# A decoder kernel on one core: transposes of the feature stage get a PSUM bank of their own, the constant fills of a scratch area are issued in another order, and the causal row maxima take one instruction

## What is computed

```python
x = x + linear_attention(layernorm(x))     # "stage 0": q, k, v projections, then
#   dd  = einsum('bhnd,md->bhnm', data * d**-0.25, proj)      m = 32 features per head
#   qf  = exp(dd_q - 0.5*|q|^2 - max over m of dd_q) + 1e-4
#   kf  = exp(dd_k - 0.5*|k|^2 - max over everything) + 1e-4
#   out = (qf @ (kf^T v)) / (qf @ sum kf)
x = x + cross_attention(layernorm(x), ctx, mask)              # "stage 1", softmax
x = x + tree_feed_forward(layernorm(x))                       # routed leaves, gathered by row
x = x + causal_attention(layernorm(x))                        # "stage 2", softmax
x = x + cross_attention(layernorm(x), ctx)                    # "stage 3", softmax
x = x + expert_layer(layernorm(x))                            # top 16 of 1024 per head
```

## Time and profile before

| | us |
|---|---|
| median of 3 runs (888.3 to 891.41) | 890.37 |
| the profiled execution | 889.77 |
| its span, first to last instruction | 887.7 |
| busy: PE 700.2 (79%), DVE 640.8 (72%), ACT 440.9 (50%), POOL 280.0 (32%) | |

### The profile page before, as it was taken

One profiled execution on the slowest core, in us unless ns is written; L12 is line 12 of the kernel. 1 busy time (PEld: TensorE's weight loads), 2 busy tenths in 40 slices (PEclk: granted clock), 3 DMA queues, 4 the chain that ended last, 5 costly groups with the idle time before them and its releaser, 6 DMA issues. The chain is left out here.

```text
span 887.7 us, 15168 instructions
## 1 busy us (share of the span) xinstructions
PE 700.2 (79%) x5016; PEld 533.6 (60%) x5016; DVE 640.8 (72%) x2791; ACT 440.9 (50%) x1051; POOL 280.0 (32%) x253
## 2 busy tenths in 40 slices
PE   3876877887657988987777588888876958888898
PEld 1435533444257767776675466555456947877788
DVE  5675547653499698976795456776449999999984
ACT  1113003465067787888762345555632556455562
POOL 3012732201333132331240111211012037677793
PEclk9887557998678999999887689988987989999999
DMA  8500051300489887997546233332000000000000
GB/s 256 139 1 2 0 72 29 41 14 1 170 326 354 328 330 266 372 401 262 207 168 166 60 44 47 48 39 39 3 1 1 1 1 2 4 4 4 7 4 7
DMA packets 42678, 93.67 MB, mean 106 GB/s; under 512 B 4050, under 2 KB 30194, under 8 KB 34408
## 3 DMA queue, kind: packets, MB, share of 16 engines
q0 software_dynamic: 9216, 69.47, 20.5%
q1 hardware_dynamic: 33384, 23.23, 13.0%
HBM read 74.42 MB, written 0.52 MB: 84 GB/s over the span
## 5 line engine op out<-in xcount | busy, mean ns | idle before, releaser
L757 ACT ACTIVATE arena<-arena,hact 128x128 f32<-128x128 f32 x512 | 155.0, 388 | 1.0
L567 POOL TENSOR_TENSOR arena<-arena 128x1024 f32<-128x1024 f32 x64 | 121.2, 1914 | 82.6 <-DVE arena L1227 65.2
L657 ACT ACTIVATE arena<-psum 128x512 f32<-128x512 f32 (+1 forms) x192 | 102.8, 561 | 86.5 <-PE psum L1377 85.4
L888 DVE TENSOR_REDUCE rowmax<-psum 128x2 f32<-128x512 f32 x128 | 82.6, 688 | 35.1 <-PE psum L1359 32.8
L1078 DVE CUSTOM_DVE_ANT_0 arena<-arena,fx 128x128 f32<-128x128 f32 x384 | 106.0, 350 | 0.3
L1700 PE MATMUL psum<-arena 128*128 128x128 f32 x688 | 87.3, 285 | 21.3 <-DVE arena L1227 19.2
L1700 PEld LDWEIGHTS psum<-arena 128*128 128x128 f32 x688 | 82.8, 199 | 24.5 <-DVE arena L1227 12.9
L1359 PE MATMUL psum<-arena 128*128 128x256 bf16 (+1 forms) x384 | 79.4, 307 | 22.6 <-DMA arena<-parts 12.3
L1589 PE MATMUL psum<-identf,arena 128*128 128x128 f32 x544 | 75.0, 292 | 25.4 <-ACT arena L757 25.2
L810 ACT ACTIVATE psum<-arena,tneg 128x1024 f32<-128x1024 f32 x64 | 71.0, 1112 | 39.7 <-POOL arena L567 14.0
L1589 PE MATMUL psum<-arena,identf 128*128 128x128 f32 x544 | 78.6, 299 | 15.4 <-ACT arena L757 14.6
(11 more groups left out here) (220 smaller groups left out, 1219.9 us busy)
## 6 DMA issues: line engine op xcount, KB each, us to landing
arena<-parts SPq DMA_DIRECT2D x144, 64.0 KB
arena<-zeros SPq DMA_DIRECT2D x6, 1232.0 KB
w_sb<-attn_w SPq DMA_DIRECT2D x1, 768.0 KB, 7.8
x<-x_in SPq DMA_DIRECT2D x1, 512.0 KB, 4.3
fx<-ctx_in SPq DMA_DIRECT2D x1, 512.0 KB, 4.9
picked<-mask_in SPq DMA_DIRECT2D x1, 512.0 KB, 6.1
wq_sb<-peer_wq SPq DMA_DIRECT2D x1, 512.0 KB, 7.9
down_sb<-table_down SPq DMA_DIRECT2D x1, 512.0 KB, 8.6
```

Source lines behind the costliest of these rows:

```text
L567: nc.gpsimd.tensor_tensor(grid[k % 3].rearrange("p (i j) -> p i j", i=PK), sim[:, t, h, :].unsqueeze(2).to_broadcast([P, PK, PK]), sim[:, ...
L657: nc.scalar.activation(probs[k % (2 * HG)][:, 0:w], bank(2 + k % 2, 0, w), ACT.Exp, scale=float(D) ** -0.5).then_inc(probs_ready, 1)
L757: a = nc.scalar.activation(w, w, ACT.Copy, scale=hact[i % 2][:, l:l + 1])
L888: i = nc.vector.tensor_reduce(rowmax[n % 2][:, :, h], bank(k % 2).rearrange("p (s n) -> p s n", s=SUB), AX.X, ALU.max)
```

## The change

1. **Feature stage.** The transposes of `eq` go to bank 6 and no longer to banks 0 and 1, in two halves of four (`turn_q(n, s)`), since one bank holds four. ACT, not VectorE, copies each half out (with the 1e-4 as the bias of the copy). The features are split into a query half (`features(n, 0)`) and a key half (`features(n, 1)`) with a semaphore each, and the query half of batch n + 1 is placed in TensorE's stream ahead of the turns of batch n: it waits for `zq` of batch n, the key half for `zk` of batch n. The transposes of the context now also wait for all turns to be copied.
2. **SP.** The ones of an area (with its zeros, in the second run) are issued ahead of that area's `place`, in place of all three behind the first `place`. Those of the third area come behind `place_max(first)`.
3. **Row maxima.** For a causal head the two reductions (128 columns; 256 columns) become one over 384 columns in three groups of 128; `max_parts` joins the second and third group with one more small instruction per causal batch.

```diff
@@ sync: run
+            def fixed(i, afresh):
+                if afresh:
+                    pad(i)
+                sp.dma_start(stk[i][KS:KM, :, 1, :], ones...).then_inc(pad_ready[i], 16)
...
-                place(first)
-                for i in range(3):
-                    if first > B and i == 1:
-                        sp.wait_ge(fh_ready, len(ORDER))
-                    if first > B and i > 0:
-                        pad((first + i) % 3)
-                    sp.dma_start(stk[(first + i) % 3][KS:KM, :, 1, :], ones...).then_inc(pad_ready[(first + i) % 3], 16)
+                fixed(first % 3, afresh)
+                place(first)
+                if afresh:
+                    sp.wait_ge(fh_ready, len(ORDER))
+                fixed((first + 1) % 3, afresh)
                 place(first + 1)
                 place_max(first)
+                fixed((first + 2) % 3, afresh)
@@ scalar: feature loop
                 act.wait_ge(zq_ready, n + 1)
                 if n >= 1:
-                    act.wait_ge(qft_ps, n)
+                    act.wait_ge(qft_ps, SUB * n)
                 nc.scalar.activation(eq, zq, ACT.Exp).then_inc(eq_ready, 1)
+                for s in range(SUB):
+                    act.wait_ge(qft_ps, SUB * n + s + 1)
+                    nc.scalar.activation(qf_t[:, SUB * n + s, :, :], bank(6).rearrange("p (g n) -> p g n", g=HG),
+                                         ACT.Copy, bias=1e-4).then_inc(qft_ready, 1)
@@ vector: row_max, max_parts
-                    nc.vector.tensor_reduce(rowmax[n % 2][:, 0, h:h + 1], bank(k % 2, 0, P), AX.X, ALU.max)
-                    i = nc.vector.tensor_reduce(rowmax[n % 2][:, 1, h:h + 1], bank(k % 2, P, P + S), AX.X, ALU.max)
+                    i = nc.vector.tensor_reduce(rowmax[n % 2][:, :, h], bank(k % 2, 0, 3 * P).rearrange("p (s n) -> p s n", n=P),
+                                                AX.X, ALU.max)
...
+                if stage(n) == 2:
+                    link(nc.vector.tensor_tensor(rowmax[n % 2][:, 1, :], rowmax[n % 2][:, 1, :], rowmax[n % 2][:, 2, :], ALU.max))
@@ vector: feature loop
-                dve.wait_ge(dd_ps, n + 1)
+                dve.wait_ge(ddq_ps, n + 1)
...
-                dve.wait_ge(qft_ps, n + 1)
-                nc.vector.tensor_scalar(qf_t[:, SUB * n:SUB * n + SUB, :, :],
-                                        psum[:, 0:2 * BANK].rearrange("p (s g n) -> p s g n", s=SUB, g=HG),
-                                        1e-4, None, ALU.add).then_inc(qft_ready, 1)
@@ tensor: feature loop (features, half_norms and turn_q hold the old instructions)
+            def features(n, w):
+                if n == 0 and w == 0:
+                    pe.wait_ge(feat_ready, 1)
                 if n >= 1:
+                    pe.wait_ge(zk_ready if w else zq_ready, n)
...
+            def turn_q(n, s):
+                pe.wait_ge(eq_ready, n + 1)
+                if n + s >= 1:
+                    pe.wait_ge(qft_ready, SUB * n + s)
+                for g in range(HG):
+                    j = (s * HG + g) * P
+                    i = nc.tensor.transpose(bank(6, g * P, g * P + P), eq[:, j:j + P], identf[:, :])
+                i.then_inc(qft_ps, 1)
+
+            features(0, 0)
+            half_norms(0)
+            features(0, 1)
+            for n in range(B):
+                if n + 1 < B:
+                    pre(n + 1)
+                    features(n + 1, 0)
+                turn_q(n, 0)
+                if n + 1 < B:
+                    half_norms(n + 1)
+                    features(n + 1, 1)
+                turn_q(n, 1)
...
             pe.wait_ge(in_ctx, 48)
             pe.wait_ge(zk_ready, B)
+            pe.wait_ge(qft_ready, SUB * B)
```

More of the change, by code:

```diff
@@ L99, in decoder_program @@
         vaug = [sb(f"vaug{i}", [P, SUB, H, VW]) for i in range(4)]
-        rowmax = [sb(f"rowmax{i}", [P, SUB, H]) for i in range(2)]
+        rowmax = [sb(f"rowmax{i}", [P, 3, H]) for i in range(2)]
         negmax = sb("negmax", [P, SUB, H])
@@ L417, in place_max @@
                 sp.dma_start(stk[n % 3][KS:KM, :, 0, :], mt[n % 2][:, :]).then_inc(max_in[n % 3], 16)
+            def fixed(i, afresh):
+                if afresh:
+                    pad(i)
+                sp.dma_start(stk[i][KS:KM, :, 1, :],
+                             ones[:, :].unsqueeze(1).to_broadcast([KM - KS, H, S])).then_inc(pad_ready[i], 16)
             def run(first, last):
-                if first == B:
+                afresh = first > B
+                if afresh:
+                    sp.wait_ge(leaf_done, len(ORDER) - 2)
+                else:
                     sp.wait_ge(consts, 1)
@@ L897, in max_parts @@
                 mp = mparts[n % 2]
[L898 removed]
+                if stage(n) == 2:
+                    link(nc.vector.tensor_tensor(rowmax[n % 2][:, 1, :], rowmax[n % 2][:, 1, :], rowmax[n % 2][:, 2, :], ALU.max))
+                link(nc.vector.tensor_scalar(negmax[:, :, :], rowmax[n % 2][:, 0:SUB, :], -1.0, None, ALU.mult))
                 link(nc.vector.tensor_copy(mp[:, :, 0, :], negmax[:, :, :]))
@@ L1414, in _, with half_norms @@
             pre_v(0)
-            for n in range(B):
+            def features(n, w):
+                if n == 0 and w == 0:
+                    pe.wait_ge(feat_ready, 1)
                 if n >= 1:
[L1417 to L1420, removed]
+                    pe.wait_ge(zk_ready if w else zq_ready, n)
                 pe.wait_ge(qk_ready, n + 1)
                 fw = feat_w[:, :, :].rearrange("p h m -> p (h m)")
-                for w in range(2):
-                    for s in range(SUB):
-                        nc.tensor.matmul(bank(2 * w + s), qk_f[n % 2][:, w, s * P:s * P + P], fw, start=True, stop=True)
+                for s in range(SUB):
+                    i = nc.tensor.matmul(bank(2 * w + s), qk_f[n % 2][:, w, s * P:s * P + P], fw, start=True, stop=True)
+                i.then_inc(dd_ps if w else ddq_ps, 1)
+            def half_norms(n):
                 pe.wait_ge(sq_ready, n + 1)
+                if n >= 1:
+                    pe.wait_ge(zk_ready, n)
                 for w in range(2):
```

17 lines of the change are left out of this document (7 added, 10 removed).

## The result

The changed kernel is slower: 897.51 us (median of 20 runs, 890.27 to 910.01) against 890.57 us (20 runs, 885.46 to 896.86), a ratio of 1.0075 with a 95% interval of 1.0053 to 1.0098. The ratio leaves out the two slowest executions of the changed kernel (904.83 and 910.01), which lie over 1.5% above its fastest. The forecast was 867.5, 861 to 878. The profiled execution took 900.37 us, with a span of 898.6, which is 10.9 more than before.

The account below looks back on a forecast made before the run. It took VectorE and TensorE, about equal in work and waiting for each other, to bound the feature loop. 15.6 + 0.9 + 6.3 + 0.2 = 23.0 us off 889.77 gave 866.8, as median 867.5; range 861 to 878.

Parts of the forecast that it names:

- the part on the row maxima: Causal heads: one reduction of 0.54 us replaces two; 0.2 us gained, between 0.9 lost and 5 won.
- rival 3: Feature loop: TensorE slow through whole batches, with the key features behind the first turn; kernel slower; chance 0.03.
- the 0.19 us of a turn: End of the feature stage: time per turn, taken as a mean of the earlier trace; four make 0.8 us.
- Feature loop: VectorE's copy and its waits go, 11.05 us per batch; 2.6 us saved in the first batch, 12.2 in later ones.
- the last batch: Feature loop: without a norm, VectorE's bias part of 2.4 us and the feature steps take 7.6 us.
- rival 1: Feature loop: TensorE becomes the bound, period about 13 us, two thirds of 12.2 lost, total 875 us; chance 0.13.
- its cover: Feature loop: TensorE is not late for VectorE; query and key maximum each have 5 us to spare.
- the lower end of 8 us: Feature stage: lower bound of its 15.6 us gain, if TensorE is mostly slow.
- End of the feature stage: After the last `zk`: ACT's copies and turns lose 1.2 us, the wait for POOL goes and gains 2.0.
- Ones ahead of the parts: First rows of n = 4: ones no longer issued behind the parts; 0.9 us gained, 0 to 1.5.
- Third area's zeros: Second run: zeros behind the maxima let rows of n = 9 start earlier; 6.3 us gained, 3.8 to 7.5.
- rival 2: Third block of zeros delays rows of n = 10 by up to 6.2 us; total 872 us; chance 0.10.

Follow-up runs that it names:

- e1: The changed kernel with an unused tile of 384 B per partition ahead of `arena`, which again starts at a multiple of 256 B: 872.72 us, ratio 0.9832.
- e2: The kernel before with an unused tile of 128 B per partition ahead of `arena`, placing it as in the changed kernel: 918.29 us, ratio 1.0348.
- e8: The changed kernel with an unused tile of 128 B ahead of `arena`, which starts at 138240, a multiple of 512 B: 871.97 us, ratio 0.9797.
- e5: The kernel before with the feature edit alone (bank 6 for the turns, ACT copies, split features), `arena` aligned: 878.07 us, ratio 0.9866.
- e4: The kernel before with `parts` moved 128 B off a multiple of 256 B and `arena` kept in place modulo 512 B: 889.25 us, ratio 0.9994.
- e3: The kernel before with an unused tile of 512 B per partition, moving `arena` but keeping its place modulo 256 B: 888.99 us, ratio 0.9992.
- e6: The kernel before with SP's new order of ones and zeros alone, `arena` aligned: 880.43 us, ratio 0.9899.
- e7: The kernel before with the row maxima edit alone and an unused tile of 384 B keeping `arena` at a multiple of 256 B: 891.24 us, ratio 1.0002.
- e9: The kernel before with `arena` moved to 32 B past a multiple of 256 B: 919.29 us, ratio 1.033.
- e10: The kernel before with `arena` moved to 224 B past a multiple of 256 B: 916.59 us, ratio 1.0297.

## Why the prediction was wrong

**The step that failed** is in the part on the row maxima. It costed the instructions (0.54 for the reduction, 0.2 in sum) and not the line of the diff that makes `rowmax` larger. That line moves `arena`, and the step's true price was not 0.2 gained but, with the move, about 25 to 29 us lost: 24.8 between e1 and the changed kernel, 28.6 in e2. With it fell the assumption behind the sum that whatever the change doesn't edit keeps its length. The pace of the parts that the sum took from the earlier trace rows was one for aligned pieces (13.45 us from first issue to first rows of n = 14 before, 15.67 after). None of the rivals had this; all five were about the order and the length of the engines' work. The one on the slower side, rival 3, meant a TensorE that is slow through whole batches, with the key features behind the first turn. No run shows that: the longest period of the kernel after is 12.55 us, at a granted clock of 0.57, and shorter than the 13.6 us of before. That the kernel came out slower all the same is no hit for it. A look at the queue's share could not have shown it, for before the change all of SP's writes into the areas are aligned, and the size of `rowmax` in the diff was the only sign.

Without the move the forecast would have stood: e1 and e8 came at 872.72 and 871.97 us, inside 861 to 878 and 4 to 5 us above the 867.5. Part of that is luck, since two misses of opposite sign meet: alone, the feature edit gave 12.5 for 15.6 and the order 10.2 for 7.2. Three readings of the working are also off, though none moves the sum by more than 0.2 us: the row maxima's 0.6 less 0.2 is 0.4 and not 0.2; the 0.19 us of a turn is busy time by count (6.1 by 32) and not the mean of the earlier trace rows, 352 ns; and a granted clock of 0.88 is not "half and half" but, with the levels 0.50 and 1.00 of these traces, about a quarter of the time at the lower. Point by point:

- **Feature loop: mechanism right, size too large.** Forecast was an end of the last `zk` at 59; it is 64.7 after, 62.1 in e1 (first `zk` 29.76, last 60.89 + 1.22), 73.8 before. The first batch gains 2.9 after (30.63 to 27.73; forecast 2.6), but only 0.9 in e1, and the middle periods of 11.99 and 11.22 (12.09 and 11.22 in e1) stand near the forecast of 11.05. The term that was mis-sized is the last batch: 7.6 forecast, 12.55 measured after, 7.82 in e1, where it took 11.07 in e8 and 10.61 in e5. That is rival 1 in one batch out of three. The stretch 47 to 60 us in the kernel after and, below, in e1 shows the two cases:

```profile
47.00:60.00 13.00, 12.53 (x32) 7.15 (x33) 10.11 (x18) 2.91 (x5) 2.38 (x7) 0.54 0.00 0
```

```profile
47.00:60.00 13.00, 8.85 (x40) 4.98 (x38) 11.58 (x24) 4.44 (x8) 3.00 (x8) 1.00 0.01 1
```

The clock is 0.54 in one and 1.00 in the other, with the same stream of instructions. TensorE did 32 matmul records in 12.5 busy us, or 40 in 8.9. In e5 the clock there was 0.61 and in e8, with its aligned `arena`, 0.68; the last `zk` ended at 62.3 and 65.1. So the address doesn't decide it. In the old loop that end varies as much, from 71.2 (e4) to 76.1 (e3). Which clock an execution gets, and why, the runs don't settle. The forecast took its cover as holding since the change takes idle time from TensorE; no run shows that less idle time brings the faster clock, and in the kernel after TensorE is busy 12.53 of 13.00 us there at 0.54. Nor does a run show the lower end of 8 us for a TensorE that is mostly slow: e5, with 0.61 in that stretch, gained 12.5 us. Among e1, e5, e8 and the changed kernel the end of the last `zk` differs by up to 3 us.
- **End of the feature stage.** The keys' exponential starts 5.2 us after the last `zk` ends (64.71 to 69.94), 4.1 in e1, for 4.5 forecast: right in size. The wait for POOL is gone, and from that exponential to the projections of n = 4 it is 25.2 us, before 27.1: 1.9 gained, forecast 2.0. In the medians the whole stage gained 12.5 us (e5) for 15.6 forecast.
- **Ones ahead of the parts: right in sign, half the size or less.** From the last issue of the parts to the first rows of n = 4 it is 6.0 us in the three kernels with the new order and an aligned `arena` (e1, e6, e8), and 6.2 to 6.4 in the five with the old one (before, e3, e4, e5, e7): 0.2 to 0.4 gained for 0.9 forecast. The forecast took the 5.6 of n = 10 as the time without ones, and that was not reached. In the changed kernel the slower transfers took more than the gain back, 8.8 us from last issue to rows.
- **Third area's zeros: mechanism right, more gained than forecast.** Rows of n = 9 come 14.1 us after those of n = 8 (forecast 14.6), even in the changed kernel with slow pieces. Rows of n = 10 follow by 19.4, forecast 21, and the wait there is 3.42 and not over 6: rival 2 did not occur. Rows of n = 8 to rows of n = 10 are 8.4 us shorter in e6, where 6.3 was forecast. The forecast's 2.5 us for parts "to start and to signal" and 2.3 for the maxima to land stand in no row, and no run shows them as such; measured is that the columns of n = 15 before start 2.65 us after the issue of their `mt` begins (633.21 to 635.86) and 1.9 after it ends. The two order edits together gave 10.2 us in the medians (e6) for 7.2 forecast.
- **Row maxima as instructions: right.** The median reduction takes 559 ns for 0.54 us forecast, and e7 is no change (1.0002).

## What to carry to other kernels

Here a diff that made two buffers larger by 64 bytes each moved `arena` by 128 bytes, and the move cost 24.8 us (the kernel after against e1) to 28.6 us (e2). So when a diff changes the size of a buffer, compare the starts of the tiles in the built programs of before and after, ahead of costing instructions. Of the tiles that have moved, note those that DMAs write in pieces as small as these (512 bytes), and compare the remainder of their start by 256: 32, 128 and 224 cost 27 to 30 us here, and 0 cost nothing (e3, 0.9992). When stretches that a change doesn't edit get longer, compare the DMA queue's share at equal packets and bytes, and put an unused tile of the offset into the old kernel: one run of it gives the price of the address alone. When parts gain and the whole loses, look for what they share, and that may be the memory layout.

## What was not expected of the hardware

The transfers from `parts` to `arena`, both in SBUF, in pieces of 512 bytes took longer in every kernel in which `arena` doesn't start at a multiple of 256 bytes: first issue to first use of twelve blocks of 64 KB (n = 14) took 13.5 us aligned (e1) and 15.6 (e2) or 15.7 (after) otherwise, and the queue's time per engine was 113 to 120 us in the eight aligned kernels (113 in e3, 120 in e8) and 135 to 141 in the others (after, e2, e9, e10). Offsets of 32, 128 and 224 bytes cost 29.95, 28.60 and 27.25 us. The start of the source, moved by 128 bytes, has no effect that could be measured (e4, 0.9994). The queue with the leaves, whose packets have a mean of 7.5 KB (69.47 MB in 9216), took 182 us per engine in the kernels before and after. That is no test of large pieces: the leaves' places in `arena` are 8256 or 8704 bytes long and lie one behind the other, so in the kernel before seven of the eight start off a multiple of 256 already, and their data come on another queue and from HBM (74.42 MB read in all in both kernels). Whether larger pieces pay is open.
